# First half of a layer: 16 products per chunk in place of 24, two sums joined by VectorE, lookups ahead

## What is computed

```python
def _propagate(all_emb, rows, cols, vals):        # 18750 x 64
    acc = all_emb
    x = all_emb
    for _ in range(3):
        x = segment_sum(vals[:, None] * x[cols], rows, num_segments=18750)
        acc = acc + x
    return acc / 4

rating = users_emb @ items_emb.T
rating = rating + bias_user[users] + bias_item.T
return sigmoid(rating)
```

## Time and profile before

| | us |
|---|---|
| runs (3), median | 7561.97 (7558.92 to 7563.39) |
| the profiled execution | 7557.79 |
| its span | 7556.0 |
| first half of layer 0, 1, 2 (inside the span) | 1393, 1231, 1231 |

### The profile page before, as it was taken

The page is one execution under the profiler, slowest core; times in us unless marked ns, Lnnn a source line. Parts: engine busy times, 40 slices in busy tenths (PEclk is TensorE's granted clock), DMA queues, the critical chain, the costliest instruction groups (busy, mean ns, idle before and its releaser), DMA issues.

```text
span 7556.0 us, 213021 instructions
## 1 busy us (share of the span) xinstructions
PE 4726.8 (63%) x73184; PEld 4198.0 (56%) x73188; DVE 5009.9 (66%) x11593; ACT 4137.8 (55%) x10708; POOL 2330.0 (31%) x2100
## 2 busy tenths in 40 slices
PE   5201111057777777887566666788666666678879
PEld 4200110046666666887556666688655666668854
DVE  9999999964444445999544444599844444469970
ACT  0155445333333335999444444699744444479976
POOL 0144434034444443000454455200055555520000
PEclk9755555555556655555676666655577776665559
DMA  9300000034444444554344444455444444445536
GB/s 345 148 0 0 0 0 0 0 94 135 133 137 134 135 134 129 142 145 120 127 138 132 136 137 137 133 145 146 110 137 138 135 138 135 134 132 145 145 105 241
DMA packets 750538, 918.14 MB, mean 122 GB/s; under 512 B 71784, under 2 KB 607881, under 8 KB 750363
## 3 DMA queue, kind: packets, MB, share of 16 engines
q1 hardware_dynamic: 658540, 665.77, 31.9%
q0 software_dynamic: 91520, 250.84, 8.9%
q10 hardware_dynamic: 434, 1.05, 0.1%
HBM read 529.36 MB, written 388.09 MB: 121 GB/s over the span
## 4 chain that ended last, share of the span: by engine, by line
PE 34%; issue 23%; DVE 17%; DMA 11%; ACT 10%; another core or an unknown queue 2%; POOL 2%; DVEq 1%; ACTq 0%; SPq 0%; POOLq 0%
PE psum L1420 28%; DMA ring<-posts 11%; ACT ring L630 5%; ACT ring L628 3%; DVE store L987 3%; DVE store L985 2%; DVE total L817 2%; DVE store L995 2%; DVE store L996 2%; POOL ring L711 2%; PE psum L1415 2%; DVE ring L1174 1%; ACT ring L627 1%; PE psum L1471 1%
## 5 line engine op out<-in xcount | busy, mean ns | idle before, releaser
L1420 PE MATMUL psum<-ring 128*128 128x64 bf16 x45504 | 2524.4, 228 | 1187.7 <-issue 1077.5
L1420 PEld LDWEIGHTS psum<-ring 128*128 128x128 bf16 x45504 | 2256.0, 121 | 1437.2 <-issue 1411.9
L618 ACT ACTIVATE ring<-psum,ring 128x64 f32<-128x64 f32 x7584 | 1654.6, 340 | 2207.2 <-DVE ring L1197 889.8
L740 POOL DMA_INDIRECT posts<-ring x1896 | 1866.9, 985 | 1968.6 <-ACT ring L618 1531.6
L1170 DVE COPY ring<-store 128x384 bf16 x1896 | 522.2, 275 | 1472.6 <-PE psum L1420 714.5
L1174 DVE TENSOR_SCALAR ring<-ring,lane_f 128x512 bf16<-128x512 bf16 x3792 | 1177.7, 352 | 0.0
L1445 PE MATMUL psum<-ring 128*128 128x64 bf16 x15168 | 1002.6, 244 | 0.0
L1445 PEld LDWEIGHTS psum<-ring 128*128 128x128 bf16 x15168 | 965.1, 167 | 0.0
L630 ACT ACTIVATE ring<-ring 128x1024 bf16<-128x1024 uint8 x948 | 943.5, 1042 | 0.0
L1439 PE MATMUL psum<-ring 128*128 128x64 bf16 x7584 | 616.9, 249 | 238.4 <-ACT psum L634 224.8
L1439 PEld LDWEIGHTS psum<-ring 128*128 128x128 bf16 x7584 | 555.8, 158 | 302.5 <-issue 300.4
(11 more groups left out here) (239 smaller groups left out, 4207.9 us busy)
## 6 DMA issues: line engine op xcount, KB each, us to landing
ring<-posts SPq DMA_DIRECT2D x474, 516.0 KB, 3.9
ring<-lanes_d SPq DMA_DIRECT2D x474, 512.0 KB
out<-ring SPq DMA_DIRECT2D x200, 250.0 KB, 2.0
posts<-store SPq DMA_DIRECT2D x2, 20640.0 KB, 115.8
posts<-store SPq DMA_DIRECT2D x2, 20124.0 KB, 88.6
posts<-ring POOLq DMA_INDIRECT x1896
ring<-runs_d SPq DMA_DIRECT2D x158, 128.0 KB
user_rows<-total SPq DMA_DIRECT2D x1, 1568.0 KB, 5.9
```

Of the source, the lines that this page charges most:

```text
L618: last = nc.scalar.activation(of, psum[:, n, b * F:(b + 1) * F], ACT.Copy, scale=vring[:, h, c * BLOCK + b:c * BLOCK + b + 1])
L740: pool.indirect_dma_start(out=posts[:, :], out_offset=bass.IndirectOffsetOnAxis(ap=dring[:, h, c:c + 1], axis=0), in_=msg[:, n, :], in_off ...
L1420: last = pe.matmul(psum[:, n, b * F:(b + 1) * F], hot[c][:, k, b * P:(b + 1) * P], xt[c][:, (k * PARTS + x) * F:(k * PARTS + x + 1) * F], ...
```

## The change

**PE.** One product of 128 columns now takes parts 0 and 1 of a tile together, and one of 64 columns takes part 2, which is added to the columns of part 1. A chunk has 16 products. A block has 128 columns of psum, in which two sums stand, and a chunk fills a whole bank. Chunk n uses bank c = n mod 4, and banks 4 and 5 are for the lookups.

**VectorE.** A new function `join` adds the two sums of a chunk and writes them to `msg`, by two reduces (L1172 of the changed kernel). It is called after the comparisons of chunk n, for chunk n - 4, so VectorE's `s_sent` wait there is the one it has passed already. It tells PE and ScalarE by `s_added`.

**ScalarE** scales `msg` in place, after `s_added`.

**Lookups.** PE does those of a half body after the last chunk of the half body before (`look_up`), and in layer 0 ahead of the loop for the first. `rhot` is made after the comparisons of c = 2 of the half body before (`run_hots`). At a half's end `place` waits for `s_looked`. The first and the last body of layer 0 stand outside the loop, and the first body of the other layers.

```diff
@@ ScalarE
-                        act.wait_ge(s_sent, i * 8 + (done + n + 5))
+                        act.wait_ge(s_added, i * 8 + (done + n + 5))
                         for b in range(BLOCK):
                             of = msg[:, n, b // 2 * HROW + b % 2 * F:b // 2 * HROW + b % 2 * F + F]
-                            last = nc.scalar.activation(of, psum[:, n, b * F:(b + 1) * F], ACT.Copy,
+                            last = nc.scalar.activation(of, of, ACT.Copy,
                                                         scale=vring[:, h, c * BLOCK + b:c * BLOCK + b + 1])
@@ VectorE
-                def send(i, first):
+                def join(sent, slot):
+
+                    dve.wait_ge(s_sent, sent)
+                    halves = psum[:, slot % 4, :].rearrange("p (a e x f) -> p a e f x", a=2, e=2, x=2)
+                    to = msg[:, slot, :].rearrange("p (a w) -> p a w", w=HROW)[:, :, 0:2 * F].rearrange("p a (e f) -> p a e f", f=F)
+                    for a in range(2):
+                        last = nc.vector.tensor_reduce(to[:, a, :, :], halves[:, a, :, :, :], AX.X, ALU.add)
+                    last.then_inc(s_added, 1)
+
+                def run_hots(h, landed, looked):
+
+                    dve.wait_ge(s_drow[h], landed)
+                    if looked is not None:
+                        dve.wait_ge(s_looked, looked)
+                    for k in range(2):
+                        last = nc.vector.tensor_scalar(rhot[h][:, k, :], runs_r[h], lane_f[:, k:k + 1], None, ALU.is_equal)
+                    last.then_inc(s_rhot, 1)
+
+                def place(i, h):
+
+                    dve.wait_ge(s_looked, i * 2 + (h + 1))
+                    nc.vector.tensor_reduce(found[:, h, :], psum[:, 4 + h, 0:4 * PARTS].rearrange("p (c x) -> p c x", x=PARTS),
+                                            AX.X, ALU.add).then_inc(s_found, 1)
+                    dve.wait_ge(s_found, i * 2 + (h + 3))
+                    nc.vector.tensor_tensor(dest_m[:, bass.ds(i * 8 + h * 4, 4)], found[:, h, :], order_m[:, bass.ds(i * 8 + h * 4, 4)],
+                                            ALU.add).then_inc(s_placing, 1)
+
+                def send(i, first, final=False):
...
                             last.then_inc(s_hots, 1)
-                            if layer == 0 and c == 0:
-                                dve.wait_ge(s_drow[h], i * 16 + 16)
-                                for k in range(2):
-                                    last = nc.vector.tensor_scalar(rhot[h][:, k, :], runs_r[h], lane_f[:, k:k + 1], None, ALU.is_equal)
-                                last.then_inc(s_rhot, 1)
+                            if not (first and h == 0):
+                                join(i * 8 + (done + n + 1), (n + 4) % 8)
+                            if layer == 0 and c == 2 and not (final and h == 1):
+                                run_hots(1 - h, i * 16 + 16 * (h + 1), None if first and h == 0 else i * 2 + h)
+                        if layer == 0:
+                            place(i, h)
                         dve.wait_ge(s_msg, i * 8 + (done + h * 4 + 4))
...
+                for n in range(4):
+                    join(done + CHUNKS + n + 1, 4 + n)
@@ PE
+                def look_up(i, h):
...
+                    pe.wait_ge(s_rhot, i * 2 + (h + 3))
+                    pe.wait_ge(s_found, i * 2 + (h + 1))
+                    for m in range(4):
+                        for k in range(2):
+                            last = pe.matmul(psum[:, 4 + h, m * PARTS:(m + 1) * PARTS], rhot[h][:, k, m * P:(m + 1) * P],
+                                             dflat[:, bass.ds(at_d[m] + k * PARTS, PARTS)], start=(k == 0), stop=(k == 1))
+                    last.then_inc(s_looked, 1)
...
                         pe.wait_ge(s_hots, i * 8 + (done + n + 9))
-                        pe.wait_ge(s_msg, i * 8 + (done + n + 1))
+                        pe.wait_ge(s_added, i * 8 + (done + n + 1))
                         for b in range(BLOCK):
                             for k in range(2):
-                                for x in range(PARTS):
-                                    last = pe.matmul(psum[:, n, b * F:(b + 1) * F], hot[c][:, k, b * P:(b + 1) * P],
-                                                     xt[c][:, (k * PARTS + x) * F:(k * PARTS + x + 1) * F],
-                                                     start=(k == 0 and x == 0), stop=(k == 1 and x == PARTS - 1))
+                                of, parts = hot[c][:, k, b * P:(b + 1) * P], xt[c][:, k * PARTS * F:(k + 1) * PARTS * F]
+                                pe.matmul(psum[:, c, b * 2 * F:(b + 1) * 2 * F], of, parts[:, 0:2 * F],
+                                          start=(k == 0), stop=False, skip_group_check=True)
+                                last = pe.matmul(psum[:, c, (2 * b + 1) * F:(2 * b + 2) * F], of, parts[:, 2 * F:3 * F],
+                                                 start=False, stop=(k == 1), skip_group_check=True)
                         last.then_inc(s_sent, 1)
+                        if layer == 0 and c == 3 and not (final and n == 7):
+                            look_up(i + n // 4, 1 - n // 4)
```

56 lines of the change are left out of this document (30 added, 26 removed).

## The result

The changed kernel takes 7399.1 us (median of 4 runs, 7387.0 to 7406.1), beside 7562.7 for the kernel before in the same session: ratio 0.978, 95% interval 0.977 to 0.979, or 164 us less. On another chip (experiment 4) the ratio was 0.983, or 124 us. The sign and the range of the prediction held; the forecast gain of 390 us did not, and 7399 lies outside the 7000 to 7350 of the forecast itself.

A forecast was written before the change was run, and what follows sets the result against it. PE's instruction feed, held back by POOL's scatters in the first halves, was taken as the bound. Gains of 140 us in layer 0 and 128 each in layers 1 and 2, less 6, gave 390: about 7170 us, range 6900 to 7500.

The forecast's parts named there:

- The reading of the bound: First halves: while POOL issues scatters, PE's instructions hardly arrive; 1078 us of PE's idle time is issue idle.
- the other 107 need 1.15 us: Layers 1 and 2, per half: 30 of 137 PE instructions arrive while closed, the rest in 1.15 us open; 7.05 us.
- The second step that failed: Layers 1 and 2: body taken as 13.8 us from PE's feed, with VectorE's floor of 12.8 hidden below it.
- Layer 0: Body falls from 17.57 to 15.8 us, PE's feed being late next above VectorE's 15.2; gain 140 us.
- VectorE's price: Two added sums per chunk at 0.335 us each; block with join 1.38 us, floor 12.8 us per body in layers 1 and 2.
- ScalarE in place: Scaling from SBUF in place of psum costs no more: 295 ns for 128 elements against 340 for 64 from psum.
- The runs for the lookups: Layer 0, SP's queue: used two blocks earlier; no wait counted, up to 0.5 us per half kept for the range.
- the slack of 2 us: Chain of join, scale, scatter, landing: landings come 2 us before VectorE asks for them, so no cost.
- A: Rival: PE's feed no longer binds; VectorE alone sets bodies of 12.8 and 15.2 us; about 6965 us, chance 0.20.
- B: Rival: dry spell is a fixed price of four scatters, some 3 us; halves stay 7.7 in layers 1 and 2; about 7530 us, 0.14.
- C: Rival: scatters come one by one, PE closed 1.8 us after each; halves of 8.3 and 8.6 us; about 7715 us, 0.11.
- D: Rival: each VectorE reduce costs its upper bound, 0.60 us; blocks of 1.91 us; about 7955 us, chance 0.05.

The follow-up runs named there:

- experiment 4: Changed kernel with the join two chunks behind in place of four: ratio 0.969 to the kernel before; rerun beside the changed kernel (0.983) on one chip: 0.971.
- experiment 1: Scatters left out, POOL only counting the semaphore up: the kernel before took 5631 us, the changed kernel 6729 us.
- (2): Kernel before with plain writes of the same rows to consecutive places instead of scatters: 6285 us issued by POOL, 6709 us issued by ScalarE.
- (6): Chips that don't starve PE: changed kernel with join three behind 6995 us, with lookups back 7021, with empty join 6651; kernel before with 96 columns 6501.
- 3: Kernel before with 16 products per chunk in place of 24, no join: 7168 us with 64 columns (beside 7439), 7177 with 96 (beside 7450).
- (7): Changed kernel with an empty join (no sums), 6670 us; kernel before with 96-column products and two idle reduces per chunk, 6896 us; neither chip starved PE.

## Why the prediction was right or wrong

**The reading of the bound** held, and more: without scatters the issue idle is gone (experiment 1). Its cause was too wide. Not every issue by POOL starves PE, only the scatter as it stands (2), and only on some chips (6).

**Layers 1 and 2, the step that failed:** "the other 107 need 1.15 us". It took the open time to be what PE's instructions need, so fewer instructions would close the gap between the groups. From all scatters of 800 us of layer 1, with PE counted as closed from a group's first start to 1.8 us after its last, a scatter comes with 1.44 us closed and 0.49 open before, and with 1.50 closed and 0.40 open after. The closed part was forecast at 5.7 / 4 = 1.43, or 5.9 / 4 = 1.48 if the scatters follow VectorE's blocks. The open part should have been 0.29 either way and fell only to 0.40: of the 1.4 us by which a body is longer than 13.8, it has some 0.9. With 96 columns and no join it is 0.18 (other chip; the changed kernel has 0.35 there). The supply rates that I used, 93 and 5 per us, came from a single pair of groups, and 3 shows 20 per us under steady scatters.

**The second step that failed** is the larger of two limits: 13.8 for the feed, 12.8 for VectorE, and nothing for PE and VectorE waiting for each other. In layer 1 of the changed kernel PE waits 80 us for the join's bank (78 in the rows of 4), 1.0 us per body, which stood in no term.

**What took the gain** is the join, with what comes with it. The same number of products per chunk gives 13.55 us per body without it and 14.70 with it on one chip, beside 14.86 before: 1.3 us won by fewer instructions, 1.15 given back. In layer 1 that is 90 us. PE is idle 42 us longer (by the rows of 4: issue idle 30 less, waits for VectorE 74 more) and busy 48 us longer (775 beside 727), at a granted clock of 0.75 in place of 0.79. The lag alone (4) and the number of columns (3) are not the cause. But the two kernels also differ in the psum banks that PE takes in turn (four, and eight), in ScalarE's source and in the shapes of the products, and none of these was undone by itself. In the trace a message goes by VectorE's block of 1.36 us after each dry spell. That this way is the mechanism, rather than VectorE's time as such or the banks, was only argued (7).

**Layer 0: the right number by luck, for a wrong reason.** 15.84 for 15.8, but I had PE's feed as what is late next. Without any scatter it still runs 15.5 (1): VectorE sets it, with waits for PE at the ends of the half bodies because PE waits for the join's bank. The lag of two takes them away and gives 15.09, where I had VectorE's floor at 15.2.

**VectorE's price** was right: 1.36 us per block (1.38), each reduce 0.33 apart with a duration of 0.416. The floor of layers 1 and 2 was 12.8; without scatters it is 11.3, as the waits around the rings that I took from the earlier trace rows were partly PE's lateness; with scatters on a chip that doesn't starve it is 12.75. By the Trainium skill (VectorE: DVE Perf Modes, the cycle table in the section on the TRN2 errata) a reduce would take 120 + 256 cycles, an estimate of 0.39 us; the trace has 0.33 from one to the next and 0.416 for one. Its advice, in the rules for kernel authors, to consider restructuring a reduce on a hot path was the better guide here.

**ScalarE in place** was not free. One operation lasts 340 ns on SBUF as from psum, but they follow each other more slowly: ScalarE is busy 2033 us with them in place of 1655, 0.20 us more per chunk, and a message has to wait for it. The prediction compared durations alone. The runs for the lookups were waited for 9 times in 1000 us of layer 0, 5.6 us in all. The landings of the scatters were waited for 3 times in 1050 us of layer 1, 6.8 us in all: the slack of 2 us was there.

**The rivals.** A's world, a feed that doesn't bind, exists on two chips, but there the kernel before gains too, and kernels with the full join lose 7 to 8%. B had the right size for layers 1 and 2 (7.7 per half, measured 7.6) with the wrong cause: the dry spells are no fixed price of four scatters, since 96 columns shorten the body. The range held only because it reached up to just below B. C is refuted: in layers 1 and 2 the groups got longer, and in layer 0, where they did get shorter (3.8 scatters to 2.0), the body fell below C's 17.2. D is refuted by the 0.33 us of a reduce.

## What to carry to other kernels

When an engine is starved in spells, don't divide its instructions by a supply rate: ask what chain of engines leads from its restart to the event that starves it again, and whether the change lengthens it. A change that pays for a scarce resource with an engine that had slack should be measured without the scarcity as well (here without scatters, +1097 us), since the scarcity may not be there on the next chip. Give a psum bank back well before its next writer wants it: moving the join from four to two chunks behind gave 1.2%, all of it in layer 0.

## What the hardware showed that I had not expected

- With an indirect scatter every 1.3 to 1.9 us PE stands still without a releaser in the profile: 1003 to 1078 us of issue idle in the kernel before, next to none with plain writes of the same 129 KB from POOL or from ScalarE's queue.
- That depends on the chip: 7433 to 7563 us for the kernel before on four sessions' chips, 6501 and 6506 on two others, where kernels with the same scatters have next to no issue idle.
- No two scatters start less than 1.26 us apart, though one takes 0.96 on POOL.
- Four scalings of 64 columns in a row take 1.07 us on SBUF; from psum they kept ScalarE busy for 0.87 (1655 us for 1896 chunks), though one lasts 340 ns from either.
- PE's instructions came at 20 per us through 63 us of steady scatters, and nearly not at all for 5 us in spells of the changed kernel (4001 to 4006). The scatters just ahead of that spell are 1.27 us apart, those of the stretch 1.6; but the spacing alone doesn't tell the two apart. Counted in layers 1 and 2 from the fourth scatter of a group on, PE starts some 3 products between two scatters that are 1.45 to 1.75 us apart in the changed kernel, and 16 in the 96-column one. What does stays open.
